# Choosing the experts tile by tile, and writing the recurrent experts' fetch slots earlier, in a two-layer graph and mixture-of-experts kernel

## The reference, cut to what matters

```
x = x + L0_gnn(layernorm(x))      # dense diffusion over a 256x256 graph
x = x + L0_ffn(layernorm(x))      # 8 experts, 2 per token: gelu(x @ we1) @ we2
x = x + L1_gnn(layernorm(x))      # 4352 edges: gather, message, sum per node, GRU
x = x + L1_ffn(layernorm(x))      # 8 one-step LSTM experts, 2 per token
```

```
logits      = ...                         # layer 0: relu(x @ gw1 + gb1) @ gw2 + gb2
                                          # layer 1: x @ router_w + router_b
top_w, top  = top_k(logits, 2)            # two experts per token
combine[t, top[t]] += softmax(...)        # their weights
out         = sum_e combine[:, e] * expert_e(x)
```

## Time and profile before

| what | value |
|---|---|
| median of 3 runs | 453.93 us |
| the profiled execution, its own time | 454.3 us |
| span of its instructions | 452.5 us |
| PE busy | 420.7 us, 93% |
| DVE busy | 388.9 us, 86% |
| ACT busy | 296.2 us, 65% |
| POOL busy | 126.0 us, 28% |
| ffn experts begin / end, about | 54.4 / 176 us |
| lstm gating ends, experts begin, about | 303.3 us |

### The profile page before, as it was taken

How to read it: one execution, slowest core, us unless ns; L and a number is a source line. 1 busy time by engine, 2 the same in 40 slices (tenths; PEclk the granted TensorE clock), 3 DMA queues, 4 the chain that set the end, 5 groups by cost and what they waited for, 6 DMA issues and landing times.

```text
span 452.5 us, 6263 instructions
## 1 busy us (share of the span) xinstructions
PE 420.7 (93%) x2241; PEld 344.1 (76%) x2241; DVE 388.9 (86%) x624; ACT 296.2 (65%) x346; POOL 126.0 (28%) x141
## 2 busy tenths in 40 slices
PE   4988999999999996997999999999999989998994
PEld 2755788888887875676998998866888778786883
DVE  6978789998899786788999996978999989898693
ACT  7966378778877762633454446569888779877551
POOL 7984000111100004148878400032001311100400
PEclk9999999999999999799999999999999999999998
DMA  7932568899998865997777425217989999988711
GB/s 235 347 100 92 187 243 314 320 341 377 374 379 311 345 225 151 392 361 222 203 227 231 123 64 204 105 51 285 390 321 324 343 401 328 357 337 307 257 45 50
DMA packets 26213, 116.20 MB, mean 257 GB/s; under 512 B 7084, under 2 KB 8268, under 8 KB 15296
## 3 DMA queue, kind: packets, MB, share of 16 engines
q1 hardware_dynamic: 18672, 93.78, 55.9%
q0 software_dynamic: 7216, 21.79, 14.9%
q10 hardware_dynamic: 288, 0.15, 0.1%
HBM read 109.15 MB, written 6.55 MB: 256 GB/s over the span
## 4 chain that ended last, share of the span: by engine, by line
PE 53%; DVE 24%; DMA 12%; ACT 5%; issue 3%; SPq 1%; POOL 1%; DVEq 0%; ACTq 0%; POOLq 0%
DVE wlo L1049 9%; PE bank L1706 9%; PE bank L1707 8%; PE bank L1713 8%; DMA xg<-node_rows,idx 6%; PE bank L2165 4%; PE bank L2167 3%; PE bank L1697 3%; PE bank L1698 3%; PE bank L1699 3%; ACT whi L723 2%; DVE wlo L1054 2%; DMA raw<-in_weights_dram 2%; DMA node_rows<-A_sb 2%; PE bank L2047 1%
## 5 line engine op out<-in xcount | busy, mean ns | idle before, releaser
L1049 DVE TENSOR_TENSOR wlo<-raw,whi 128x2048 fp32r<-128x2048 f32 x72 | 163.0, 2286 | 14.9 <-ACT whi L723 14.7
L723 ACT ACTIVATE whi<-raw 128x2048 fp32r<-128x2048 f32 x73 | 138.3, 1915 | 7.3 <-PE bank L2134 5.2
L1706 PE MATMUL bank<-whi,xe_hi 128*128 128x512 f32 (+1 forms) x200 | 78.0, 393 | 1.0 <-ACT xe_hi L756 0.7
L1707 PE MATMUL bank<-wlo,xe_hi 128*128 128x512 f32 (+1 forms) x200 | 76.0, 383 | 0.0
L666 POOL DMA_INDIRECT xg<-node_rows,idx x14 | 19.9, 1422 | 140.8 <-DVE idx L1344 140.8
L1713 PE MATMUL bank<-whi,xe_lo 128*128 128x512 f32 (+1 forms) x200 | 51.9, 381 | 0.2 <-DVE xe_lo L1337 0.2
L699 POOL DMA_INDIRECT gath<-node_rows,src_i x34 | 44.0, 1293 | 15.0 <-DVE mp L1617 8.3
L1706 PE MATMUL bank<-whi,hT_hi 128*128 128x512 f32 (+1 forms) x124 | 46.9, 385 | 0.7 <-ACT hT_hi L786 0.4
L1707 PE MATMUL bank<-wlo,hT_hi 128*128 128x512 f32 (+1 forms) x124 | 45.0, 369 | 0.0
L1706 PEld LDWEIGHTS bank<-whi,xe_hi 128*128 128x128 f32 x200 | 37.6, 188 | 8.9 <-ACT xe_hi L756 0.9
L1707 PEld LDWEIGHTS bank<-wlo,xe_hi 128*128 128x128 f32 x200 | 37.7, 188 | 7.1
(11 more groups left out here) (327 smaller groups left out, 875.3 us busy)
## 6 DMA issues: line engine op xcount, KB each, us to landing
raw<-in_weights_dram SPq DMA_DIRECT2D x85, 1024.0 KB, 6.9
y_rows<-y_sb POOLq DMA_DIRECT2D x16, 256.0 KB, 6.4
ea<-in_ea_dram SPq DMA_DIRECT2D x8, 256.0 KB, 4.2
node_rows<-xn POOLq DMA_DIRECT2D x4, 256.0 KB, 2.4
gath<-node_rows,src_i POOLq DMA_INDIRECT x34, 4.0
x<-in_x_dram SPq DMA_DIRECT2D x1, 512.0 KB, 3.8
gw<-in_L_ffn_gw_dram SPq DMA_DIRECT2D x1, 512.0 KB, 9.1
node_rows<-A_sb POOLq DMA_DIRECT2D x2, 256.0 KB, 5.9
```

The lines of the kernel that those rows point to most:

```text
L723: act.activation(whi[n % SPL][:, :, :], raw[n % RAW][:, :, :], ACT.Copy).then_inc(hi_cut, 1)
L1049: dve.tensor_tensor(wlo[n % SPL][:, :, :], raw[n % RAW][:, :, :], whi[n % SPL][:, :, :].bitcast(f32), ALU.subtract).then_inc(lo_cut, 1)
L1706: pe.matmul(ps, xh[:, blocks + k, :], whi[w % SPL][:, k, cs], start=first and k == 0, stop=False)
L1707: pe.matmul(ps, xh[:, blocks + k, :], wlo[w % SPL][:, k, cs], start=False, stop=False)
```

## The change: what it does

1. Both gatings run on DVE tile by tile: `lg`, `top`, `topi`, `oh`, `mask`, `penal` of tile 0, then of tile 1 (every step linked), so `oh`, `mask`, `penal` and `posm` are two half-size instructions each. PE's `positions` is split by tile and writes to banks 1 and 2; the counts are a function of their own. The `keep_busy` of the ffn gating is 3 + 3 instead of 6, and the 3 before `gather_first` are gone.
2. `slots_of(n)` follows for both tiles: `posm` of the tile and G of expert 0 for the tile (this replaces `build_g(0)`). In lstm, `xn_lo` of tile 1 (`low_tokens`) stands between the two. `low` (ffn, with the semaphore `shift`) and `tw` (lstm, `d`) now come after `slots_of(1)`.
3. `gather_first` on PE runs over tile 0 first (8 matmuls, waiting for G of tile 0 alone), then tile 1; `turn_g(1)` is done after the first half of tile 1's matmuls instead of after all 16. DVE does `slots(1)` ahead of both `xe_first`.
4. In the recurrent layer `slots(e+2)` moves in step e from after `xe_one(e+1)` to right after the product of line 1409, ahead of the cut that follows. In step 0 it moves from after that cut to before it. In ffn those stay where they were.

```diff
--- before.py
+++ after.py
@@ -436,7 +436,7 @@
         ffn, lstm = Run("ffn", 0), Run("lstm", 1)
         gate = {n: sem(f"gate_{n}") for n in (
             "hid_ps", "hid_sb", "lg_ps", "shift", "exp", "d", "dexp", "mask", "pos_ps", "route", "comb3",
-            "combT", "more", "xn_cut", "split")}
+            "combT", "more", "xn_cut", "split", "first_g")}
 
         g0 = {n: sem(f"g0_{n}") for n in ("hot", "used", "cnt", "turn_ps", "adj", "h_ps", "xT_hi",
                                           "h", "h_hi", "h_lo", "wh", "u_ps", "ra", "ra_hi", "ra_lo",
@@ -1236,13 +1236,28 @@
                         link(dve.scalar_tensor_tensor(out=lg[:, n, :], in0=B[6 + n][:, 0:E], scalar=rstd[:, n:n + 1],
                                                       in1=gb[:, 1, :], op0=ALU.mult, op1=ALU.add))
                     link(dve.max(top[:, n, :], lg[:, n, :]))
-                    ins = dve.max_index(topi[:, n, :], top[:, n, :], lg[:, n, :])
-                link(ins)
-                link(dve.tensor_tensor(oh[:, :, :, :],
-                                       iota_t[:, 0:E].unsqueeze(1).unsqueeze(1).to_broadcast([P, NT, 2, E]),
-                                       topi[:, :, 0:2].unsqueeze(3).to_broadcast([P, NT, 2, E]), ALU.is_equal))
-                dve.tensor_tensor(mask[:, :, :], oh[:, :, 0, :], oh[:, :, 1, :], ALU.add)\
-                   .then_inc(gate["mask"], 1)
+                    link(dve.max_index(topi[:, n, :], top[:, n, :], lg[:, n, :]))
+                    link(dve.tensor_tensor(oh[:, n, :, :], iota_t[:, 0:E].unsqueeze(1).to_broadcast([P, 2, E]),
+                                           topi[:, n, 0:2].unsqueeze(2).to_broadcast([P, 2, E]), ALU.is_equal))
+                    dve.tensor_tensor(mask[:, n, :], oh[:, n, 0, :], oh[:, n, 1, :], ALU.add)\
+                       .then_inc(gate["mask"], 1)
+                    dve.wait_ge(gate["mask"], NT * (nth - 1) + n + 1)
+                    link(dve.tensor_scalar(penal[:, n, :], mask[:, n, :].bitcast(f32), -1000.0, 1000.0,
+                                           ALU.mult, ALU.add))
+
+                def slots_of(n):
+                    dve.wait_ge(gate["pos_ps"], (NT + 1) * (nth - 1) + n + 1)
+                    link(dve.tensor_tensor(posm[:, n, :], B[1 + n][:, POS:POS + E], penal[:, n, :], ALU.add))
+                    ins = dve.tensor_scalar(G[:, 0, n, 0, :], iota_t[:, 0:P], posm[:, n, 0:1], None, ALU.is_equal)
+                    if n == 0:
+                        ins.then_inc(gate["first_g"], 1)
+                    else:
+                        ins.then_inc((ffn if nth == 1 else lstm).g_built, 1)
+
+                slots_of(0)
+                if nth == 2:
+                    low_tokens(5, slice(1, NT))
+                slots_of(1)
                 if nth == 1:
                     dve.tensor_tensor(low[:, :, 0:E], lg[:, :, :], top[:, :, 0:1].to_broadcast([P, NT, E]),
                                       ALU.subtract)
@@ -1250,17 +1265,9 @@
                        .then_inc(gate["shift"], 1)
                 else:
                     dve.tensor_tensor(tw[:, :, 0], top[:, :, 1], top[:, :, 0], ALU.subtract).then_inc(gate["d"], 1)
-                dve.wait_ge(gate["mask"], nth)
-                link(dve.tensor_scalar(penal[:, :, :], mask[:, :, :].bitcast(f32), -1000.0, 1000.0, ALU.mult, ALU.add))
-
-                if nth == 2:
-                    low_tokens(5, slice(1, NT))
-                dve.wait_ge(gate["pos_ps"], 2 * nth - 1)
-                ps = B[6][:, POS:POS + NT * E].rearrange("p (n e) -> p n e", n=NT)
-                link(dve.tensor_tensor(posm[:, :, :], ps, penal[:, :, :], ALU.add))
 
             def overflow(nth):
-                dve.wait_ge(gate["pos_ps"], 2 * nth)
+                dve.wait_ge(gate["pos_ps"], (NT + 1) * nth)
                 dve.tensor_scalar(over[:, :], B[7][:, POS:POS + E], float(P), None, ALU.is_gt)\
                    .then_inc(gate["route"], 1)
 
@@ -1408,9 +1415,10 @@
                         dve.wait_ge(run.gates, run.gated(e) + 2)
                         dve.tensor_tensor(act3[:, 0, :], act3[:, 0, :], act3[:, 1, :], ALU.mult)\
                            .then_inc(run.h_ok, 1)
+                        if e + 2 < E:
+                            slots(e + 2)
                         if e == 0:
                             cuts(run.chunk("in", e, 0) + SPL + 1)
-                            slots(2)
                         elif e < E:
                             cuts(run.chunk("in", e, 1) + SPL + 1)
                         if run.halved(e):
@@ -1450,11 +1458,10 @@
                     more_link(dve.tensor_tensor(sel_more[:, job:job + 1], sel_m[:, 0:1], sel_m[:, 1:2], ALU.max))
                     build_g(e)
 
-                build_g(0)
                 overflow(run.layer + 1)
                 build_g(1)
+                slots(1)
                 xe_first(0)
-                slots(1)
                 xe_first(1)
                 if run.layer == 0:
                     choice_weights()
@@ -1470,7 +1477,7 @@
                     results(step)
                     if step + 1 < E:
                         xe_one(step + 1)
-                        if 3 <= step + 2 < E or step == 0 and run.layer == 0:
+                        if step + 2 < E and run.layer == 0:
                             slots(step + 2)
                     else:
                         with dve.If(number > 0):
@@ -1815,15 +1822,17 @@
                 ins.then_inc(g0["u_ps"], 1)
 
 
-            def positions(nth):
-                pe.wait_ge(gate["mask"], nth)
-                ps, counts = B[6][:, POS:POS + 2 * E], B[7][:, POS:POS + E]
-                pe.matmul(ps[:, 0:E], tri[:, 0:P], mask[:, 0, :], start=True, stop=True)
-                pe.matmul(ps[:, E:2 * E], tri[:, P:T], mask[:, 0, :], start=True, stop=False)
-                pe.matmul(ps[:, E:2 * E], tri[:, 0:P], mask[:, 1, :], start=False, stop=True)\
-                  .then_inc(gate["pos_ps"], 1)
-                pe.matmul(counts, tri[:, P:T], mask[:, 0, :], start=True, stop=False)
-                pe.matmul(counts, tri[:, P:T], mask[:, 1, :], start=False, stop=True).then_inc(gate["pos_ps"], 1)
+            def positions(nth, n):
+                pe.wait_ge(gate["mask"], NT * (nth - 1) + n + 1)
+                ps = B[1 + n][:, POS:POS + E]
+                if n == 1:
+                    pe.matmul(ps, tri[:, P:T], mask[:, 0, :], start=True, stop=False)
+                pe.matmul(ps, tri[:, 0:P], mask[:, n, :], start=n == 0, stop=True).then_inc(gate["pos_ps"], 1)
+
+            def counts(nth):
+                ps = B[7][:, POS:POS + E]
+                pe.matmul(ps, tri[:, P:T], mask[:, 0, :], start=True, stop=False)
+                pe.matmul(ps, tri[:, P:T], mask[:, 1, :], start=False, stop=True).then_inc(gate["pos_ps"], 1)
 
             def ffn_gating():
                 turn_x(1, (0,))
@@ -1845,8 +1854,11 @@
                         ins = pe.matmul(B[6 + n][:, 0:E], hid[:, k, n * P:(n + 1) * P], gw2[:, k, :],
                                         start=k == 0, stop=k == 1)
                     ins.then_inc(gate["lg_ps"], 1)
-                keep_busy(B[0], 6)
-                positions(1)
+                keep_busy(B[0], 3)
+                positions(1, 0)
+                keep_busy(B[0], 3)
+                positions(1, 1)
+                counts(1)
 
             def lstm_logits(n):
                 pe.wait_ge(xt_sb, 3 * NT + n + 1)
@@ -1864,8 +1876,10 @@
                 turn_x(3, (1,))
                 keep_busy(B[0], 3)
                 lstm_logits(1)
+                positions(2, 0)
                 keep_busy(B[0], 6)
-                positions(2)
+                positions(2, 1)
+                counts(2)
 
             def turn_comb(nth):
                 pe.wait_ge(gate["comb3"], nth)
@@ -1900,15 +1914,22 @@
                     return G[:, (e // 2) % 2, n, e % 2, :]
 
                 def gather_first():
-                    pe.wait_ge(run.g_built, 1)
-                    for k in range(KB):
-                        ps = quarters(B[6 if k < KB // 2 else 4])[:, k % (KB // 2), :]
-                        for n in range(NT):
-                            pe.matmul(ps, xn_hi[:, n, k * P:(k + 1) * P], columns(0, n), start=n == 0, stop=False)
+                    for n in range(NT):
+                        if n == 0:
+                            pe.wait_ge(gate["first_g"], run.layer + 1)
+                        else:
+                            pe.wait_ge(run.g_built, 1)
+                        for k in range(KB):
+                            ps = quarters(B[6 if k < KB // 2 else 4])[:, k % (KB // 2), :]
+                            pe.matmul(ps, xn_hi[:, n, k * P:(k + 1) * P], columns(0, n),
+                                      start=n == 0 and k % (KB // 2) == 0, stop=False,
+                                      skip_group_check=True)
                             ins = pe.matmul(ps, xn_lo[:, n, k * P:(k + 1) * P], columns(0, n),
```

(10 more changed lines are left out.)

## The result

The changed kernel took 456.11 us (median of 22 executions, 452.48 to 461.07) against 454.23 us of the kernel before (22 executions, 450.88 to 458.37): a ratio of 1.0048 with a 95% interval of 1.0026 to 1.0069. That is 1.2 to 3.1 us slower, where 1.0 us faster was forecast. The three executions that the prediction had before it (453.8 to 454.97) spread far less than the kernel does. The ratio leaves out slow executions, of the changed kernel the two at 460.11 and 461.07.

A forecast was written before the change was run, and what follows sets the result against it. PE was taken as full in the ffn experts, with late token-row fetches and loads near their limit in lstm. Ffn +0.85, lstm gains and costs, and loads +0.6 total -1.05: 453.25 us, 452.9 on the median's scale, range 452.2 to 453.6.

The forecast's parts named there:

- Part 1: Ffn gating: gather neither starts nor ends earlier, ScalarE gets `low` late, first product 1.0 us later; +0.85 for the layer.
- Fetches 5 and 7: Lstm steps: earlier slots issue these token-row fetches sooner, so PE's waits for them go, -1.5 and -1.1 us.
- The cost of the earlier slots: Lstm: DVE waits for `turn_g` behind line 1409, costing 0.25 us in step 1, 0.4 each in steps 4 and 5.
- ACT late in the ffn gating: Ffn gating: ACT waits for the later `low`, then rounds for 1.90 us, so the first product begins 1.0 us later.
- +0.85: Ffn layer's loss in us, PE's 0.4 us of idle time swallowing part of the 1.0; ends 0.5 and 1.1.
- lstm gating -0.45: Lstm gating: DVE starts the two cuts at 303.64 instead of 304.09, a gain of 0.45 us, ends 0.2 and 0.7.
- fetch 1 -0.5: Lstm, expert 1's token rows: fetch issued 1.1 us earlier, so its 0.5 us of lateness goes.
- 2.8 us on POOL for each later lstm fetch: Lstm: each `idx` is soon followed by a cut, so issuing each fetch was counted at 2.8 us on POOL.
- The reading of rows 10: Issuing a fetch takes POOL 1.07 us if started before DVE's cut, 2.77 if a cut was running; read as blocking.
- The loads' limit: Lstm after 360 us: DMA engines busy 0.99 leave little room, so 0.6 us of gains is given back, ends 0 and 1.6.
- Rival 3: Lstm: the new wait binds DVE to PE in every step, 1.15 us each in steps 1 to 3; 455.5 us, chance 0.12.

The follow-up runs named there:

- only lstm gating: Kernel before with the lstm gating tile by tile alone, ffn gating and slots of later experts as before: 453.53 us, ratio 0.9995.
- more matmuls: Changed kernel with the ffn gating's unread matmuls at 4, 5 and 1 instead of 3, 3 and 0, `low` left late: 454.57 us, ratio 1.0025.
- both remedies: Changed kernel with `low` back ahead of both selection matrices and the ffn gating's unread matmuls at 4, 5 and 1: 452.93 us, ratio 0.9998.

## Why the prediction was wrong

Two steps failed, and either would have been enough to turn the sign of -1.05.

- **The clock: the term that was missing.** Part 1 of the prediction said of the removed `keep_busy` that they "were hidden behind G anyway" and counted PE's new gaps at nothing but their length. The changed gating was followed by the lower clock in most executions: 1.3 us in the first profile, 2.3 to 2.6 in the two others (14.51 and 14.83 against 12.19), 2.0 us on the mean by the estimate above.
- **Fetches 5 and 7, -1.5 and -1.1: mis-sized.** The mechanism holds (with the earlier slots the step to expert 5 is 13.86 to 13.88 in all nine traces, it no longer varies), but the lateness it removes stood in one of five traces with the old slots. Against 13.73 to 13.93 in the other four the step to expert 5 wins nothing, and the step to expert 7 goes from 12.81 to 13.18 up to 13.21 to 13.62. One profile was taken for the rule; no view of it could tell that.
- **The cost of the earlier slots, 0.25 in step 1 and 0.4 in steps 4 and 5:** right. DVE's waits of 1.14 and 1.18 stand against 1.15 forecast, PE is held by 0.17, 0.22 and 0.33. Against the four usual traces with old slots the steps to experts 3, 6 and 7, which follow `turn_h` of steps 1, 4 and 5, grow by about 0.4, 0.3 and 0.3. With nothing won from fetches 5 and 7 this 1.1 us is all that the earlier slots do, and it cancels the gain of the lstm gating. That is why the kernel with the ffn gating as before comes out level (0.9993).
- **ACT late in the ffn gating, +1.0, nothing swallowed:** right in size. 0.94 in the first profile, 0.93 where the clock held; the ffn experts took 73.07 to 73.09 in every trace, so the +0.85 with part swallowed was a little low. Not all of it is the place of `low`, as Part 1 had it: with `low` first 0.38 remained, by DVE's longer chain.
- **lstm gating -0.45 and fetch 1 -0.5:** right when the clock holds, 13.76 against 14.78, and fetch 1's issue took 1.05 us on POOL instead of 2.86. In one of three it was lost to a fall.
- **2.8 us on POOL for each later lstm fetch:** right in the first trace; all six took 2.75 to 3.37. In the changed kernel's second trace the last took 0.97.
- **The reading of rows 10** left out a row of the same trace: fetch 5 started 0.37 us ahead of its cut and still took 3.49.
- **The loads' limit, +0.6:** seen, at little cost. ACT waits for `raw` 4.6 us in all from 300 us on, against none in the earlier trace rows's trace, and the steps do not lengthen by it in a way I could separate.
- Rival 3 (slower, at 455.5) had the sign and came nearest to 456.1. Its wait is real, but it costs 0.4 in step 1 and next to nothing in steps 2 and 3 (13.42 us to expert 4 with old and new slots alike, 13.86 to 13.88 against 13.73 to 13.93 to expert 5), not 1.15 in each; the part that is real was in the forecast's sum already.

## What to carry to other kernels

Matmuls that nobody reads are part of a schedule: when a stretch of small operations gets longer or is cut in pieces, look again for PE's gaps in it, up to the moment that the next dense product starts, and for waits on other engines in that piece too. Whether they cost the clock takes many executions to tell. A wait that an in-order engine meets ahead of a long instruction must be judged by that instruction: `low`, 0.2 us of DVE work, moved a rounding of 1.9 us onto the path. And a transfer's lateness in one trace can be chance; before it is made a term of a sum, a second profile of the same kernel is worth more than a closer look at the first.

## What the runs showed of the hardware

- Gaps of PE of 0.3 to 0.7 us between the logits and the first product were followed by 3 to 7 us at a granted clock of 0.50 in 6 of 7 traces, and by none in the seventh with the same gating. In the kernel with matmuls ahead of the first product these did not help: the clock had fallen, four of them took 1.93 us instead of 1.02, and the product came later.
- The clock also falls ahead of the change. In six of the 14 traces (before's third, the changed kernel's first and third, only lstm gating, more matmuls, both remedies) the granted clock was 0.50 to 0.74 in each 2 us between 35 and 39 us, and these enter the ffn gating at 50.13 to 50.54 us. Seven of the eight others enter it at 49.27 to 49.54; the eighth, the changed kernel's second, enters it at 51.56 with the clock at 1.00 there, for a reason that stays open. The 22 executions of each kernel spread over 7.5 and 8.6 us.
- POOL's issue of an expert's indirect fetch takes 0.94 to 1.28 us when DVE does small work or stands still, also where one of DVE's 2.3 us subtractions (both inputs in SBUF) starts with it or later. It takes 2.7 to 3.4 when such a subtraction has been running for 0.07 to 0.37 us. Two cases stand against a simple rule: fetch 5 with the old slots starts 0.36 to 0.37 us ahead of the subtraction and takes 3.48 to 3.49 in all five traces, and one fetch that started 0.04 us into a subtraction took 0.97. The page "SBUF — State Buffer" of the Trainium skill ("Who interferes with whom") infers that a tensor_tensor leaves descriptor writing alone. The long issues don't fit that by itself, but the fetch also reads `idx` from SBUF, which the page says does contend with such an instruction; no run here separates the two.
